# One-pass float32r probabilities times context for two or three of twelve tiles, in a cross-attention kernel on Trainium2

## The reference, cut to what matters

```python
kv = context @ Wkv
k, v = jnp.split(kv, 2, axis=-1)
q = layernorm(x) @ Wq
dots = jnp.einsum('bhnd,bhmd->bhnm', q, k) * SCALE        # 8 x 16 x 56 x 1500
dots = dots - (1.0 - mask)[:, None, :, None] * MASK_NEG
attn = jax.nn.softmax(dots, axis=-1)
out = jnp.einsum('bhnm,bhmd->bhnd', attn, v) ...
x = x + out @ Wout + bout
x = x + ffn(layernorm(x))      # expert e for batch e: 128 -> 512, gelu, -> 128
```

## Time and profile before

| | |
|---|---|
| median of 3 runs | 388.45 us (387.89 to 388.56) |
| the profiled execution: its time | 387.53 us |
| its span, from the first to the last instruction | 385.9 us |
| busy: PE | 376.2 us |
| busy: DVE | 300.1 us |
| busy: ACT | 222.8 us |
| busy: POOL | 75.9 us |
| mean granted TensorE clock | 0.997 of the full 2.4 GHz |

### The profile page before, as it was taken

One profiled execution on the slowest core, in us unless ns is written; L12 is line 12 of the kernel. 1 busy time (PEld: TensorE's weight loads), 2 busy tenths in 40 slices (PEclk: granted clock), 3 DMA queues, 4 the chain that ended last, 5 costly groups with the idle time before them and its releaser, 6 DMA issues.

```text
span 385.9 us, 5472 instructions
## 1 busy us (share of the span) xinstructions
PE 376.2 (97%) x1673; PEld 271.6 (70%) x1673; DVE 300.1 (78%) x476; ACT 222.8 (58%) x294; POOL 75.9 (20%) x68
## 2 busy tenths in 40 slices
PE   7999999999999999999999999999999999999995
PEld 7667776677767776777667876777767776776674
DVE  5887778987798679987898679987998679465453
ACT  3546455775577446775577355775577455846421
POOL 0803400810082001800090001800180000000000
PEclk9999999999999999999999999999999999999998
DMA  7665020350035000333035002151031000300000
GB/s 251 214 186 141 2 80 1 83 157 1 1 84 153 8 0 11 90 130 125 0 94 145 0 0 62 55 164 72 19 93 47 0 0 8 109 0 2 3 2 3
DMA packets 23686, 25.00 MB, mean 65 GB/s; under 512 B 1240, under 2 KB 20600, under 8 KB 23672
## 3 DMA queue, kind: packets, MB, share of 16 engines
q1 hardware_dynamic: 20648, 19.45, 16.6%
q0 software_dynamic: 3024, 5.38, 5.3%
HBM read 24.59 MB, written 0.23 MB: 64 GB/s over the span
## 4 chain that ended last, share of the span: by engine, by line
PE 81%; DVE 11%; issue 5%; ACT 1%; DVEq 0%; ACTq 0%
PE ps_a L431 31%; PE ps_s L403 26%; PE ps_x L439 9%; PE ps_x L467 5%; DVE ex_sum L793 3%; DVE chunk_max L796 2%; PE ps_a L380 2%; PE ps_x L487 2%; PE ps_x L496 1%; DVE shift_diag L807 1%; PE ps_s L548 1%; PE ps_x L417 1%; PE ps_x L454 1%; PE ps_x L455 1%; DVE hid L884 1%
## 5 line engine op out<-in xcount | busy, mean ns | idle before, releaser
L431 PE MATMUL ps_a<-ex,ctx_sb 125*128 125x448 f32 x384 | 171.1, 541 | 0.0
L796 DVE TENSOR_REDUCE chunk_max<-ps_x 128x1 f32<-128x500 f32 x168 | 111.0, 676 | 29.3 <-PE ps_x L439 26.3
L625 ACT ACTIVATE ex<-ps_s 125x896 f32<-125x896 f32 x96 | 88.0, 917 | 70.3 <-PE ps_s L403 68.9
L793 DVE TENSOR_TENSOR ex_sum<-ex_sum,ex 125x896 f32<-125x896 f32 x80 | 91.9, 1149 | 5.0 <-ACT ex L625 3.7
L630 ACT COPY ps_s<-shift_row 125x896 f32<-125x896 f32 x94 | 85.6, 911 | 16.9 <-DVE shift_row L920 14.4
L431 PEld LDWEIGHTS ps_a<-ex,ctx_sb 125*128 125x128 f32 x384 | 71.4, 190 | 27.2 <-issue 21.2
L403 PE MATMUL ps_s<-qk_hi,ctxt_hi 128*125 128x448 f32 x192 | 87.1, 535 | 0.0
L439 PE MATMUL ps_x<-ctxt_hi,qk_hi 128*128 128x500 f32 x168 | 84.0, 503 | 1.3 <-DVE chunk_max L796 1.0
L403 PEld LDWEIGHTS ps_s<-qk_hi,ctxt_hi 128*125 128x125 f32 x192 | 35.9, 187 | 35.1 <-issue 35.0
L403 PE MATMUL ps_s<-qk_hi,ctxt_lo 128*125 128x448 f32 x192 | 54.8, 366 | 0.0
L403 PE MATMUL ps_s<-qk_lo,ctxt_hi 128*125 128x448 f32 x192 | 54.7, 366 | 0.0
(11 more groups left out here) (87 smaller groups left out, 259.1 us busy)
## 6 DMA issues: line engine op xcount, KB each, us to landing
ctxt_raw<-in_ctx_t SPq DMA_DIRECT2D x8, 750.0 KB, 7.7
ctx_sb<-in_ctx SPq DMA_DIRECT2D x8, 750.0 KB
ctxt_hi<-in_ctx_t POOLq DMA_DIRECT2D x21, 250.0 KB, 3.2
w_sb<-in_w SPq DMA_DIRECT2D x4, 512.0 KB, 3.8
w_sb<-in_w SPq DMA_DIRECT2D x8, 256.0 KB, 4.5
ex<-in_wq_t SPq DMA_DIRECT2D x2, 256.0 KB, 3.7
ex<-in_wk_t SPq DMA_DIRECT2D x2, 256.0 KB, 4.1
att_n<-in_wv_t SPq DMA_DIRECT2D x1, 512.0 KB, 6.1
```

The source lines that it names most:

```text
L431: mm = nc.tensor.matmul(ps_a[:, c, 0:CH], ctx_sb[0:MT, u, t, :], ex[0:MT, t % RING, c * CH:(c + 1) * CH], start=(t == 0), stop=(t == TM - 1))
L625: nc.scalar.activation(half(ex[0:MT, slot, :]), src, ACT.Exp, scale=SCALE).then_inc(ex_ready, 1)
L793: nc.vector.tensor_tensor(dst, left, ex[0:MT, t % RING, :], ALU.add).then_inc(ex_summed, 1)
L796: nc.vector.tensor_reduce(chunk_max[:, k, t:t + 1], filled()[:, 0:MC], AX.X, ALU.max).then_inc(job_free, 1)
```

## The change

For tiles 4 and 6 of every batch, and for tile 8 too in the odd-numbered ones (1, 3, 5, 7), probabilities times context is made from three rounded products like the scores. ScalarE rounds the probabilities (`ex_high_part`, 896 columns, behind the tile's exponential and seed) and the context tiles (`ctx_high_parts`, 128 columns each, at t = 2); GpSimd makes the two rests (`ex_low_part`, `ctx_low_part`); TensorE runs six one-pass matmuls in place of two float32 ones. A split tile changes places with the tile behind it in the order of use (`PV_ORDER`), so it is used one slot later, and ScalarE's wait for a free place in the ring follows that order. GpSimd's remaining work moves to earlier entries of its list, and the FFN's hidden tiles share the memory of `w_qk`.

```diff
-    CTXT_LO_AT, QK_LO_AT = [2, 6, 7], [2, 3]
+    CTXT_LO_AT, QK_LO_AT = [1, 2, 3], [1, 2]
...
+    SPLIT = [[4, 6], [4, 6, 8]]
+    SPLIT_IN_ROUND = len(SPLIT[0]) + len(SPLIT[1])
+    PV_ORDER = [[0, 1, 2, 3, 5, 4, 7, 6, 8, 9, 10, 11], [0, 1, 2, 3, 5, 4, 7, 6, 9, 8, 10, 11]]
+    CTX_HI_AT = 2
...
-        hid = sb("hid", [P, 2 * FT, TOK])
+        hid = w_qk[:, 0:4, :].rearrange("p j (a n) -> p (j a) n", n=TOK)
...
+                if t in SPLIT[b.parity]:
+                    n = SPLIT[b.parity].index(t)
+                    pe.wait_ge(ctx_lo_ready, split_at(b, n + 1))
+                    pe.wait_ge(ex_lo_ready, split_at(b, n + 1))
+                    for term, (a, e) in enumerate([(ctx_hi, ex_hi), (ctx_hi, ex_lo), (ctx_lo, ex_hi)]):
+                        if term == 2 and between is not None:
+                            between()
+                        for c in range(2):
+                            mm = nc.tensor.matmul(ps_a[:, c, 0:CH], a[0:MT, n, :], e[0:MT, n, c * CH:(c + 1) * CH],
+                                                  start=False, stop=False)
+                    mm.then_inc(pv_done, 1)
+                    return
...
-                wait(act, pv_done, b.at(TM, t - RING + 1))
+                wait(act, pv_done, b.at(TM, read_by(b, t - RING) if t >= RING else read_by(b.later(-1), t - RING + TM) - TM))
...
+            def ex_high_part(b, n):
+
+                t = SPLIT[b.parity][n]
+                act.wait_ge(ex_ready, b.at(TM, t + 1))
+                nc.scalar.copy(ex_hi[0:MT, n, :], ex[0:MT, t % RING, :]).then_inc(ex_hi_ready, 1)
+
+            def ctx_high_parts(b):
+
+                act.wait_ge(ctx_in[b.parity], b.at_every_other(16, 16))
+                for n, t in enumerate(SPLIT[b.parity]):
+                    nc.scalar.copy(ctx_hi[0:MT, n, :], ctx_sb[0:MT, b.parity, t, :]).then_inc(ctx_hi_ready, 1)
...
+                    if t == CTX_HI_AT:
+                        ctx_high_parts(b)
+                    if t in SPLIT[b.parity]:
+                        ex_high_part(b, SPLIT[b.parity].index(t))
...
+            def ctx_low_part(b, n):
+                pool.wait_ge(ctx_hi_ready, split_at(b, n + 1))
+                nc.gpsimd.tensor_tensor(ctx_lo[0:MT, n, :], ctx_sb[0:MT, b.parity, SPLIT[b.parity][n], :],
+                                        ctx_hi[0:MT, n, :].bitcast(F32), ALU.subtract).then_inc(ctx_lo_ready, 1)
+
+            def ex_low_part(b, n):
+                pool.wait_ge(ex_hi_ready, split_at(b, n + 1))
+                nc.gpsimd.tensor_tensor(ex_lo[0:MT, n, :], ex[0:MT, SPLIT[b.parity][n] % RING, :], ex_hi[0:MT, n, :].bitcast(F32),
+                                        ALU.subtract).then_inc(ex_lo_ready, 1)
...
+                    if t == CTX_HI_AT + 1:
+                        for n in range(len(SPLIT[b.parity])):
+                            ctx_low_part(b, n)
+                    if t - 1 in SPLIT[b.parity]:
+                        ex_low_part(b, SPLIT[b.parity].index(t - 1))
```

More of the change, by code:

```diff
@@ L169, in xattn_ffn @@
         ex_sum = sb("ex_sum", [P, 2, Q])
+        ex_hi = sb("ex_hi", [P, 3, Q], F32R)
+        ex_lo = sb("ex_lo", [P, 3, Q], F32R)
+        ctx_hi = sb("ctx_hi", [P, 3, D], F32R)
+        ctx_lo = sb("ctx_lo", [P, 3, D], F32R)
         shift_diag = sb("shift_diag", [P, QT, P], F32R)
@@ L207, in xattn_ffn @@
         z_t = sb("z_t", [P, P])
-        hid = sb("hid", [P, 2 * FT, TOK])
-        hid_u = sb("hid_u", [P, 2 * FT, TOK])
-        hid_e = sb("hid_e", [P, 2 * FT, TOK])
+        hid = w_qk[:, 0:4, :].rearrange("p j (a n) -> p (j a) n", n=TOK)
+        hid_u = w_qk[:, 4:8, :].rearrange("p j (a n) -> p (j a) n", n=TOK)
+        hid_e = w_qk[:, 8:12, :].rearrange("p j (a n) -> p (j a) n", n=TOK)
         out_sb = sb("out_sb", [P, D])
@@ L238, in xattn_ffn @@
         scores_ready, ex_ready = sem("scores_ready"), sem("ex_ready")
+        ex_hi_ready, ex_lo_ready = sem("ex_hi_ready"), sem("ex_lo_ready")
+        ctx_hi_ready, ctx_lo_ready = sem("ctx_hi_ready"), sem("ctx_lo_ready")
         ex_summed, pv_done, att_ready = sem("ex_summed"), sem("pv_done"), sem("att_ready")
@@ L249, in xattn_ffn, with read_by, split_at @@
         block = stack.enter_context(nc.Block())
+        def read_by(b, t):
+            return PV_ORDER[b.parity].index(t) + 1
+        def split_at(b, k):
+            before = (b.off // 2) * SPLIT_IN_ROUND + (len(SPLIT[0]) if b.parity else 0)
+            return before + k if b.i is None else b.i * SPLIT_IN_ROUND + (before + k)
         def half(t):
@@ L417, in shift_rows, with probs_ctx @@
                 return nc.tensor.matmul(dst, ones_r[:, 0:rows], diag[:, c * CH:(c + 1) * CH], start=start, stop=True)
-            def probs_ctx(b, t, between=None):
-                u = b.parity
+            def probs_ctx(b, slot, between=None):
+                u, t = b.parity, PV_ORDER[b.parity][slot]
                 pe.wait_ge(ex_ready, b.at(TM, t + 1))
-                if t == 0:
+                if slot == 0:
                     pe.wait_ge(ctx_in[b.parity], b.at_every_other(16, 16))
@@ L431, in probs_ctx @@
                     mm = nc.tensor.matmul(ps_a[:, c, 0:CH], ctx_sb[0:MT, u, t, :], ex[0:MT, t % RING, c * CH:(c + 1) * CH],
-                                          start=(t == 0), stop=(t == TM - 1))
+                                          start=(slot == 0), stop=(slot == TM - 1))
                 mm.then_inc(pv_done, 1)
```

## The result

The changed kernel takes 394.27 us (median of 6 runs, 391.59 to 394.83) against 388.38 for the kernel before on the same chip (6 runs, 387.76 to 389.05). The ratio is 1.0116, 95% interval 1.0085 to 1.0146: slower by 1.2%, clear of the noise. The ratios are those on record, worked out from the single runs, and not quotients of the medians, from which they differ by up to 0.4%: 394.27 / 388.38 is 1.0152, or +5.9 us, while 1.0116 is +4.5 us, and its interval reaches from +3.3 to +5.7. The forecast was 391.2, and at most 394.0, from 388.45. The ratio applied to 388.45 gives 393.0, inside that range; the median of 394.27 lies 0.3 above its end. The profiled execution took 394.06 us with a span of 392.3, against 385.9 before: 6.4 more.

A forecast was written before the change was run, and what follows sets the result against it. PE was taken to bound the early part of each batch, DVE the late part that prepares a next one. +1.1 + 2.8 - 0.26 - 0.78 = +2.8 us gave 391.2 us from the 388.45 median, range 385.5 to 394.0.

The forecast's parts named there:

- Odd batches: Three batches: `ex_low` of tile 8 holds DVE's addition of tile 5 by 0.92 us, nothing absorbs it: +2.8 us.
- Even batches: Three batches: `ex_low` of tile 6 delays an addition and drain, so job (8, 0) streams 0.36 us later: +1.1 us.
- Batch 0: Tile 6: the addition is late, but the next job needing that drain comes after its end; the saving stays, -0.26 us.
- Batches 6 and 7 together: An even batch's +0.36 us, and the last batch, where PE is the bound and three split tiles save 0.78.
- Tile 6 in odd batches: Job (8, 1) waits for the late drain of (7, 2): 0.24 of the 0.26 us saved is lost.
- the roundings on ScalarE: One rounding of 896 columns per split tile, 0.94 us, covered by ACT's 1.6 us of idle before an exponential: no cost.
- tile 4: All batches: the addition of tile 3 ends about 0.5 us late, paid for by DVE's 0.51 of idle before (6, 0).
- a saving at t = 9 and 11: Batches 0 to 6: these places lie where DVE sets the pace; PE only arrives earlier and waits longer: nothing.
- Hidden: Rival: no addition is held up, savings count where PE is the bound: -2.6 us, 385.8; chance 0.18.
- full saving: Rival: DVE's runs shrink with PE, so the whole saving counts: -5.2 us, 383.2; chance 0.07.
- Mild sharing: Rival: an addition under `ex_low` takes only 0.43 us more: +0.4 us, 388.8; chance 0.10.
- The heavier loss: Rival: `ex_low` of tile 8 slips behind tile 5's addition and holds the row maxima: +5.2 us, 393.6; chance 0.13.

The follow-up runs named there:

- e11: e2 with each `ex_low` made as two GpSimd subtractions of 448 columns instead of one of 896: 392.20 us, ratio 1.0082 to the kernel before.
- e4: e2 without `ex_low`; the middle term multiplies `ex_hi` a second time: 386.00 us, ratio 0.9909 to the kernel before.
- e2: The changed kernel with a guard: GpSimd's first `ctxt_lo` waits for all three context casts: 392.17 us, ratio 1.0074 to the kernel before.
- e10: The changed kernel with 11 warm-up products (`keep_clock`) in place of 10, without the guard: 392.21 us, ratio 1.0083 to the kernel before.
- e9: The changed kernel as it is, measured again: 393.32 us, ratio 1.0111 to the kernel before.
- e3: e2 with tile 8 not split, tiles 4 and 6 split in all batches: 389.20 us, ratio 0.9999 to the kernel before.
- e5: e2 with split tiles multiplied in float32 on PE as before, roundings and subtractions kept: 394.16 us, ratio 1.0140 to the kernel before.
- e7: e2 with DVE's additions of tiles 4 and 5 moved to (6, 1) and (8, 1): 386.76 us, ratio 0.9946 to the kernel before.
- e6: e2 with tiles 4 and 5 split in every batch, in their own order, none else: 384.61 us, ratio 0.9909 to the kernel before.
- e12: e6 with 11 warm-up products (`keep_clock`) in place of 10: 384.92 us, ratio 0.9890 to the kernel before.
- e8: e1 with DVE's additions of tiles 4 and 5 moved to (6, 1) and (8, 1): 390.39 us, ratio 1.0034 to the kernel before.
- e1: The kernel before with GpSimd's first `ctxt_lo` waiting for all three context casts: 388.19 us, ratio 0.9978 to the kernel before.

## Why the prediction was right, and where its size was off

**The mechanism and the sign were right.** The forecast was that an addition which arrives during `ex_low` ends 0.96 after it. The rows of the changed kernel give 0.95 and 0.94; e11 shows that it is the end of the running instruction that counts; e4 shows that without `ex_low` the kernel would be 2.6 us faster than before (388.60 to 386.00). The difference of e2 and e4, 6.2 us, is the whole price of the hold-ups. That the median of 394.27 lies above the 394.0 of the range is not the mechanism's doing but mostly that of the start, which is taken up below: e2, e10 and e11, with the same loop or nearly the same and no late run, are at 392.2.

**The terms, with e9's profile against before's.** Odd batches: predicted +2.8, measured 1.09 + 1.11 + 1.12 = +3.3. Even batches: +0.36 each, measured +0.55 and +0.48. Batch 0: -0.26, measured -0.25. Batches 6 and 7 together: 0.36 - 0.78 = -0.42, measured -0.38, a number that the scatter of the end makes weak. The sum is +3.7 where +2.8 was predicted. The range that the prediction gives for its own case has a slip: 391.2 and the +1.6 of a longer `ex_low` make 392.8, not 393.3.

**The mis-sized term is the length of `ex_low`.** I took 2.0 us; undisturbed it takes 2.10 to 2.13. I had drawn a line through two rows only 52 columns apart (1.15 us for 448, 1.24 for 500), by which 448 more columns cost 0.78, 1.93 in all, and rounded it up. They cost 0.97. The start of the one at tile 8 before the addition's arrival was predicted as 0.96, and it was 103.39 - 102.44 = 0.95. So the hold-up is 1.17 + 0.95 - 1.08 = 1.04, where 1.17 is what is left of `ex_low`, against the 0.92 predicted, and likewise 0.13 more in the even batches (an addition of 1.73, where the 0.52 predicted makes 1.60). Six batches make 0.7 of the 0.9 that were missing. The same rule of the Trainium skill ("SBUF — State Buffer", Who interferes with whom) that was weighed before, a hold-up that grows with GpSimd's instruction, agrees: the hold-up was 1.04 with 896 columns, of which 1.17 us were left when the addition arrived, and 0.09 with 448, of which 0.23 were left.

**Places that were priced at nothing.** Tile 6 in odd batches, the roundings on ScalarE, the `ctx_low` parts and tile 4: e3's odd batches are 0.06 to 0.10 above before's, so together they cost at most that. That a saving at t = 9 and 11 is worth nothing was right: PE's wait at (10, 2) grew from some 0.2 to 1.01 us. The wait says so for odd batches, and e5 for even ones.

**The rivals.** Hidden and full saving fell with e2 and e4: the additions are held, and even without `ex_low` the time is 386.00, not 383.2. Mild sharing fell with the 2.12 us of an addition and with e11. The heavier loss asked for `ex_low` to begin behind the addition of tile 5; it began 0.95 before it in the changed kernel. In e7 and e11 `ex_low`, or its second half, does run behind the addition, and there the row maxima are held, by 0.82 and 0.62.

**What the prediction did not have: the start.** Of the +5.9 of the medians the body explains 3.7 to 4.0. The rest is that 4 of the 6 runs of the changed kernel in that first measurement were late (7 of 12 in both), and none of the 6 runs of before was, though 23 of 63 later ones were. I took the scatter of three runs (0.7 us) for the scatter of the kernel. For runs without a profile the mean granted clock tells more than the time alone. Of before's 23 late runs 19 have 0.996 or less, and none of the 40 others has; of the changed kernel's 7 late runs 5 have, and none of the 5 others. So most late runs spent some time at the lower clock level, as the profiled one did from 14 us on; its start is 0.8 us later than that of e9 (19.62 against 18.78), which has the held casts without it. Where the others spent it no profile shows. Among the runs whose clock is on record, 24 of 81 without the guard (before, the changed kernel, e10) have 0.996 or less, and 8 of 89 with it. That points at the held casts as one cause of the late runs, but the kernels differ in more than the guard, so it isn't shown. Whether the change makes late starts more frequent stays open: no instruction of the start differs, and 7 of 12 against 23 of 69 decides nothing.

## What to carry to other kernels

Before work goes to GpSimd because it is idle, lay its instructions on the timeline of VectorE and look which of VectorE's instructions that read SBUF arrive in them; put them beside reductions from PSUM, which aren't held (e6), or where VectorE has slack. Then ask which place of the order the saved TensorE time reaches: the same split gained 4 us at tiles 4 and 5 and lost 4 at 4, 6 and 8. And when a kernel moves by about 1%, compare the pieces of two traces, since a start that differs by 2.4 us between runs of one program can be about half as large as the change.

## What the runs showed of the hardware

- The hold-up is that of the whole instruction, and the size of the held one does not matter: 7 columns took 0.99 us beside an `ex_low`, in place of 0.17. It goes in both directions: a GpSimd subtraction of 448 columns took 1.81 us behind an addition, in place of 1.15. A reduction from PSUM beside `ex_low` kept its 0.68.
- Not only instructions with two SBUF operands are held. The cast of the start (1.47 us in place of 0.41) reads one, and so does L943 in the last batch of the changed kernel, which takes 2.22 us in place of the 0.29 that it takes before:

```profile
362.96 2.36 POOL L1143 TENSOR_TENSOR ex_lo<-ex,ex_hi 125x896 fp32r<-125x896 f32 x1 [3.43 <-ACT ex_hi L667]
363.25 2.22 DVE L943 TENSOR_SCALAR w_qk<-w_qk 128x256 f32<-128x256 f32 x1
```

- A held instruction ends sooner after the one that holds it than its own length would say: 0.94 to 0.96 us for an addition of 1.08, 0.02 for the one of 0.17, 0.15 for the one of 0.29. Some 0.13 to 0.15 us of each passed during the wait.
- The starts in the profile do not always tell which of two is held. The first `ctxt_lo` starts 0.16 us before the third cast in both kernels: in the changed one (10.61 and 10.77) the cast is held, in the one before (10.14 and 10.30) it keeps its 0.41, and `ctxt_lo` takes 1.68 in place of 1.35.
- One GpSimd subtraction of 896 columns takes 2.10 to 2.13 us, 448 take 1.15, and 128 columns (`ctx_low`) from 0.45; the mean of the twenty `ctx_low` is 0.84, in which waits for VectorE are contained.
- TensorE's pace at the start differs between executions. Its first weight products (L372, L353 before, 16 records) took 1.16 us in seven of the profiles, 1.27 and 1.28 in e11 and e9, 1.67 in e12, 1.84 in e8, and 2.08 in e4, e5 and e7. The timeline of e2, and then that of e5:

```profile
6.09 1.16 PE L372 MATMUL ps_a<-ex 64*128 64x128 f32 x16 [0.26 <-DMA ex<-in_wk_t]
...
8.50 2.01 PE L392 MATMUL ps_s<-inv_sum,w_qk 128*128 128x112 f32 x16 [0.99 <-ACT w_qk L769]
```

```profile
6.38 2.08 PE L372 MATMUL ps_a<-ex 64*128 64x128 f32 x16 [0.54 <-DMA ex<-in_wk_t]
...
9.71 3.73 PE L392 MATMUL ps_s<-inv_sum,w_qk 128*128 128x112 f32 x16 [0.85 <-ACT w_qk L761]
```

The same products take 2.08 and 3.73 us in place of 1.16 and 2.01, 1.8 to 1.9 times as long, although the windows give a granted clock of 1.00 in both. That this is TensorE's lower clock level, 1.2 GHz against 2.4, is an estimate from these ratios. It makes 2.6 us, and the starts of e4, e5 and e7 (20.7 to 21.2 in the table) are late by about that against those of e2 and e3. Before the slow products TensorE had stood idle for 0.54 us in e5, 0.76 in e7 and 0.92 in e4, against 0.26 in e2. Idle time alone doesn't explain them: e1 has 1.16 after 0.44 us of idle time, and e8 and e12 have 1.84 and 1.67 after none. The cause stays open.
